# Self attention stacks as six transfers of 4 KB pieces in place of twelve of 1 KB

## What is computed

```python
def _L0_attn_ref(x, w_attn, w_proj):       # causal
    q, k, v = heads of (x @ w_attn.T)      # (8, 16, 512, 16)
    att = softmax(where(causal, q k^T / 4, -inf))
    return (att v, heads merged) @ w_proj.T

def _L1_attn_ref(x, qkv_w, proj_w, proj_b, q_norm_w, k_norm_w):
    q, k, v = heads of (x @ qkv_w.T)
    q, k = _rmsnorm(q, q_norm_w), _rmsnorm(k, k_norm_w)   # over the 16 of a head
    att = softmax(q k^T / 4)
    return (att v, heads merged) @ proj_w.T + proj_b
x = x + _L0_attn_ref(_layernorm(x), ...)
...
x = x + _L1_attn_ref(_layernorm(x), ...)
```

## Time and profile before

| | |
|---|---|
| median of 3 runs | 2481.39 us (2476.7 to 2486.93) |
| the profiled execution | 2478.18 us, its span 2476.3 us |
| granted TensorE clock, mean | 0.968 |
| TensorE busy | 2249.2 us (91%), 13992 matmuls |
| VectorE busy | 1413.6 us (57%) |
| ScalarE busy | 1188.7 us (48%) |
| GpSimd busy | 743.6 us (30%) |
| DMA | 197.00 MB in 160823 packets, 121104 of them under 2 KB |

### The profile page before, as it was taken

The page is one execution under the profiler, slowest core; times in us unless marked ns, Lnnn a source line. Parts: engine busy times, 40 slices in busy tenths (PEclk is TensorE's granted clock), DMA queues, the critical chain, the costliest instruction groups (busy, mean ns, idle before and its releaser), DMA issues. The chain is left out here.

```text
span 2476.3 us, 44303 instructions
## 1 busy us (share of the span) xinstructions
PE 2249.2 (91%) x13992; PEld 1427.4 (58%) x13993; DVE 1413.6 (57%) x3651; ACT 1188.7 (48%) x2803; POOL 743.6 (30%) x848
## 2 busy tenths in 40 slices
PE   7999999878996799899999999889985899999998
PEld 5444554344655567643333333345553799999997
DVE  4676666435874444577777777366654543434343
ACT  1666666623442463267777776533322433333332
POOL 3111111033531321233322321055430533333333
PEclk9999999989998899999999999999998999999999
DMA  6344444214221310323333333110009221222221
GB/s 162 104 131 124 130 125 125 65 39 136 83 78 43 102 53 1 90 76 103 106 94 105 99 100 99 41 33 10 10 3 375 66 38 32 38 33 37 35 36 23
DMA packets 160823, 197.00 MB, mean 80 GB/s; under 512 B 27238, under 2 KB 121104, under 8 KB 160528
## 3 DMA queue, kind: packets, MB, share of 16 engines
q1 hardware_dynamic: 145008, 175.47, 22.8%
q0 software_dynamic: 13680, 17.84, 4.5%
q10 hardware_dynamic: 1968, 1.60, 0.5%
HBM read 124.83 MB, written 70.12 MB: 79 GB/s over the span
## 5 line engine op out<-in xcount | busy, mean ns | idle before, releaser
L485 ACT ACTIVATE self_probs<-self_score_ps 128x512 f32<-128x512 f32 (+3 forms) x1024 | 479.6, 516 | 261.9 <-PE self_score_ps L856 151.9
L653 DVE TENSOR_REDUCE self_neg_max<-self_max_ps 128x1 f32<-128x512 f32 x512 | 328.6, 685 | 125.8 <-PE self_max_ps L842 122.2
L842 PE MATMUL self_max_ps<-self_k_stack,self_q_stack 96*128 96x512 bf16 (+3 forms) x1024 | 348.9, 343 | 32.9 <-DVE self_neg_max L650 21.8
L853 PE MATMUL self_score_ps<-self_q_stack,self_k_stack 99*128 99x512 bf16 (+3 forms) x1024 | 346.0, 345 | 13.4 <-ACT self_probs L485 13.2
L2758 ACT ACTIVATE x_stream<-experts_up_ps,experts_bias_now 128x128 f32<-128x128 f32 x568 | 161.9, 368 | 351.7 <-PE experts_up_ps L2970 351.7
L650 DVE CUSTOM_DVE_ANT_0 self_masked<-self_max_ps,self_later 128x128 f32<-128x128 f32 (+3 forms) x512 | 234.8, 488 | 128.0 <-PE self_max_ps L842 120.4
L2970 PEld LDWEIGHTS experts_up_ps<-experts_tileT,x_stream 128*128 128x128 f32 x2272 | 267.4, 194 | 5.2 <-issue 1.7
L2970 PE MATMUL experts_up_ps<-experts_tileT,x_stream 128*128 128x128 f32 x2272 | 267.8, 277 | 1.3 <-DVE x_stream L2880 1.3
L2980 PE MATMUL experts_down_ps<-experts_down,x_stream 128*128 x1136 | 256.8, 379 | 0.0
L853 PEld LDWEIGHTS self_score_ps<-self_q_stack,self_k_stack 99*128 99x128 bf16 x1024 | 99.3, 98 | 248.4 <-ACT self_probs L485 181.0
L867 PE MATMUL self_out_ps<-self_probs,self_values 128*32 128x512 f32 (+3 forms) x2048 | 235.1, 531 | 6.7 <-ACT self_o_raw L471 4.8
(11 more groups left out here) (339 smaller groups left out, 3783.9 us busy)
## 6 DMA issues: line engine op xcount, KB each, us to landing
self_parts_dram<-self_parts SPq DMA_DIRECT2D x64, 384.0 KB, 2.7
self_q_stack<-self_parts_dram SPq DMA_DIRECT2D x384, 64.0 KB, 2.3
self_k_stack<-self_parts_dram SPq DMA_DIRECT2D x360, 64.0 KB, 2.3
self_out_dram<-self_o_raw SPq DMA_DIRECT2D x60, 256.0 KB, 2.1
crossx_out_dram<-crossx_o_raw SPq DMA_DIRECT2D x16, 512.0 KB, 2.7
experts_up<-moe_up_dram SPq DMA_DIRECT2D x8, 1024.0 KB, 8.7
experts_down<-moe_down_dram SPq DMA_DIRECT2D x8, 1024.0 KB, 10.7
self_o_now<-self_out_dram SPq DMA_DIRECT2D x30, 256.0 KB
```

What stands on the lines that cost most here:

```text
L485: act.activation(probs[:, i % 8, 0:w], score_ps[:, (16 * n + i) % 3, 0:w], ACT.Exp).then_inc(exp_done, 1)
L653: dve.tensor_reduce(neg_max[:, n % 2, t, h:h + 1], max_ps[:, i % 2, 0:w], AX, ALU.max, negate=True).then_inc(max_read, 1)
L842: last = pe.matmul(max_ps[:, i % 2, 0:w], q_stack[0:ROWS, h, P * t:P * t + P], k_stack[0:ROWS, h, 0:w], start=True, stop=True)
L853: last = pe.matmul(score_ps[:, m % 3, 0:w], k_stack[0:KROWS, head, P * j:P * j + P], q_stack[0:KROWS, head, S - w:S], start=True, stop=not ...
```

## The change

In `lay_out` the columns of the q and k weights of both self attentions are put into the order depth, then head, within each 128 features, as the mixture of depths has them; self1's gains are repeated accordingly. The DRAM scratch is now part, feature, token. Then four heads of one depth lie together, 4 x 512 bf16 = 4 KB, and one transfer can fill three blocks of 16 rows. For q these are parts 0, 1, 2, then 0, 1, then 0; for k part 0 three times, part 1 twice, part 2 once, where the source is one part repeated along a new outermost dimension. The `stacked` semaphores count 96 an item. In self1 the sum of squares over a head can no longer use `head_ones`, whose ones are for neighbouring features; two VectorE instructions make a matrix `same_head` from the identity.

```diff
-        scratch = nc.dram_tensor(f"{name}_parts_dram", [4, P, 3, S], BF16).ap()
+        scratch = nc.dram_tensor(f"{name}_parts_dram", [4, 3, P, S], BF16).ap()
...
+        def stack_rows(half, g, which):
+
+            stk, item = (q_stack, k_stack)[which], 2 * half + which
+            heads = slice(GH * (g % 2), GH * (g % 2) + GH)
+            for r, count in ((0, 3), (3, 2), (5, 1)):
+                dst = stk[HD * r:HD * (r + count), GH * g:GH * g + GH, :].rearrange("r h t -> r (h t)")
+                if which == 0:
+                    yield dst, scratch[item, 0:count].rearrange("c (d h) t -> (c d) h t", h=8)[:, heads]
+                else:
+                    one = scratch[item, 3 - count].rearrange("(d h) t -> d h t", h=8)[:, heads].rearrange("d h t -> d (h t)")
+                    yield dst, one.unsqueeze(0).to_broadcast([count, HD, GH * S])
...
-                        wait(sp, stacked[2 * half], 192 * b)
-                        wait(sp, stacked[2 * half + 1], 192 * b)
-                        sp.dma_start(scratch[item], parts[:, item]).then_inc(parts_stored[half], 16)
+                        wait(sp, stacked[2 * half], 96 * b)
+                        wait(sp, stacked[2 * half + 1], 96 * b)
+                        sp.dma_start(scratch[item].rearrange("c p t -> p c t"), parts[:, item]).then_inc(parts_stored[half], 16)
...
-                    rows = slice((g % 2) * 64, (g % 2) * 64 + 64)
-                    for stk, item, which in ((q_stack, 2 * half, Q_PART), (k_stack, 2 * half + 1, K_PART))[0:2 if both else 1]:
-                        for r, part in enumerate(which):
-                            sp.dma_start(stk[HD * r:HD * r + HD, GH * g:GH * g + GH, :],
-                                         scratch[item, rows, part, :].rearrange("(h d) t -> d h t", d=HD)
-                                         ).then_inc(stacked[g], 16)
+                    for which in range(2 if both else 1):
+                        for dst, src in stack_rows(half, g, which):
+                            sp.dma_start(dst, src).then_inc(stacked[g], 16)
...
+                if norm:
+                    dve.tensor_reduce(one_head[:], c.ident[:].rearrange("p (d h) -> p h d", h=8), AX, ALU.max).then_inc(same_head_made, 1)
+                    dve.wait_ge(same_head_made, 1)
+                    dve.tensor_copy(same_head[:].rearrange("p (d h) -> p d h", h=8),
+                                    one_head[:].unsqueeze(1).to_broadcast([P, HD, 8])).then_inc(same_head_made, 1)
                 layer_norm(0, range(TT))
...
-                    pe.matmul(general[:, bank("s", b, i)], c.head_ones[:], squares[:, i % 2], start=True, stop=True).then_inc(ss_full, 1)
+                    pe.wait_ge(same_head_made, 2)
+                    pe.matmul(general[:, bank("s", b, i)], same_head[:], squares[:, i % 2], start=True, stop=True).then_inc(ss_full, 1)
...
-        "l0_qk": np.ascontiguousarray(qkv0[:, :2 * D]), "l0_v": np.ascontiguousarray(qkv0[:, 2 * D:]),
+        "l0_qk": np.ascontiguousarray(qkv0[:, mod_order[:2 * D]]), "l0_v": np.ascontiguousarray(qkv0[:, 2 * D:]),
...
-        "l1_qg": np.tile(a["L1_attn_q_norm_w"], P // HD).reshape(P, 1),
+        "l1_qg": np.repeat(a["L1_attn_q_norm_w"], P // HD).reshape(P, 1),
```

More of the change, by code:

```diff
@@ L149, in self_attention @@
             bias = sb("bias", [P, D])
-        scratch = nc.dram_tensor(f"{name}_parts_dram", [4, P, 3, S], BF16).ap()
+            one_head = sb("one_head", [P, 8])
+            same_head = sb("same_head", [P, P])
+        scratch = nc.dram_tensor(f"{name}_parts_dram", [4, 3, P, S], BF16).ap()
         out_scratch = nc.dram_tensor(f"{name}_out_dram", [2, 2 * GH, 2, HD, S], F32).ap()
@@ L177, in self_attention @@
         v_full, v_copied = sem("v_full"), sem("v_copied")
+        same_head_made = sem("same_head_made")
         e_full, x_biased, x_done = sem("e_full"), sem("x_biased"), sem("x_done")
@@ L543, in stack_keys @@
                     act.wait_ge(parts_stored[0], 32)
-                    for r, part in enumerate(K_PART):
-                        act.dma_start(k_stack[HD * r:HD * r + HD, GH * g:GH * g + GH, :],
-                                      scratch[1, 64 * g:64 * g + 64, part, :].rearrange("(h d) t -> d h t", d=HD)).then_inc(stacked[g], 16)
+                    for dst, src in stack_rows(0, g, 1):
+                        act.dma_start(dst, src).then_inc(stacked[g], 16)
                 transposed(0, 0)
@@ L838, in max_tile @@
                     if i == 0:
-                        pe.wait_ge(stacked[g], 192 * b + 192)
+                        pe.wait_ge(stacked[g], 96 * b + 96)
                     wait(pe, max_read, 16 * n + i - 1)
@@ L3043, in lay_out @@
         "x": a["x"],
-        "l0_qk": np.ascontiguousarray(qkv0[:, :2 * D]), "l0_v": np.ascontiguousarray(qkv0[:, 2 * D:]),
+        "l0_qk": np.ascontiguousarray(qkv0[:, mod_order[:2 * D]]), "l0_v": np.ascontiguousarray(qkv0[:, 2 * D:]),
         "l0_o": t(a["L0_attn_w_proj"]),
-        "l1_qk": np.ascontiguousarray(qkv1[:, :2 * D]), "l1_v": np.ascontiguousarray(qkv1[:, 2 * D:]),
+        "l1_qk": np.ascontiguousarray(qkv1[:, mod_order[:2 * D]]), "l1_v": np.ascontiguousarray(qkv1[:, 2 * D:]),
         "l1_o": t(a["L1_attn_proj_w"]), "l1_ob": np.tile(a["L1_attn_proj_b"], (P, 1)),
@@ L3059, in lay_out @@
         "moe_down": np.ascontiguousarray(a["L1_ffn_w_down"].transpose(0, 2, 1)), "moe_bu": np.ascontiguousarray(a["L1_ffn_b_up"].reshape(8, -1, P).transpose(2, 0, 1)), "moe_bd": np.tile(a["L1_ffn_b_down"].reshape(1, 8, D), (P, 1, 1)),
-        "l1_qg": np.tile(a["L1_attn_q_norm_w"], P // HD).reshape(P, 1),
-        "l1_kg": np.tile(a["L1_attn_k_norm_w"], P // HD).reshape(P, 1),
+        "l1_qg": np.repeat(a["L1_attn_q_norm_w"], P // HD).reshape(P, 1),
+        "l1_kg": np.repeat(a["L1_attn_k_norm_w"], P // HD).reshape(P, 1),
     }
```

## The result

The changed kernel is slower: 2516.71 us as the median of 4 runs (2501.8 to 2526.15), against 2479.91 us (2476.7 to 2486.93) for the kernel before in the same comparison. The ratio is 1.0138, with a 95% interval of 1.0096 to 1.018. The forecast was 2490 us with a range up to 2515, and 0.40 for slower by over 0.5%. So the sign of its sum (+9.0 us) was right, its size was a quarter of the measured +36.8 us, and the median lies 1.7 us above the range.

What follows compares the result with a forecast made beforehand. Compute paces both self attentions; late transfers cost 7 us (third groups), 1.6 (first opening) and 0.4 (second attention), +9.0 us on 2478.18, or 2490 us for a median. The range was 2474 to 2515 us.

Steps and rivals of the forecast that it cites:

- What bounds the kernel: Both self attentions: paced by compute, TensorE busy 94% and 98%; transfers matter only where one comes late, at three places.
- k's transfers on few engines: Stack loads: k's repeated source runs on as many engines as copies, so last data come 1.8 us later.
- The third group: First self attention, items 1 to 6: shift behind the stack 1.6 us late for TensorE, 9.6 us, taken as 7.
- From first issue to last data are 866.9 - 857.43 = 9.5 us: Time of a group's six stack transfers, read from the mixture of depths, against 7.7 us before the change.
- each piece takes a tenth more beside this stage's other traffic: Third group's upper end: k's 6.0 us become 6.6, twice in a row; 2.8 us an item, 17 us for six.
- The deduction for catching up: Third group: ScalarE and VectorE catch up during a stall, TensorE then waits less for them, so 9.6 us becomes 7.
- Openings and second attention: First opening +1.6 us, stores issued 3.7 us earlier; second attention's opening +0.4, its group 6 shift holding with 1.5 us.
- The first two engines become the bound: Rival, chance 0.16: pieces a fifth slower make each item over 4 us late; 20 to 45 us, 2512 us.
- its second sign: First-two-engines rival: the stacks of group 12 also come late for their maxima.
- the forecast's own case: First attention's third group 2 to 17 us late in all; chance 0.50, more than half of it under 12.4 us.
- Hidden anyway: Rival, chance 0.24: SP's 2.8 us and free engines offset k's delay, third group keeps its margin; -3 to +3 us, 2481.
- Fewer, larger transfers win: Rival, chance 0.10: gain at the opening's 4.86 us wait plus DMA waits and catching up; -6 us, 2475.

## Why the prediction was right and wrong

**What bounds the kernel: right.** Both attentions are paced by compute, and the loss began with transfers that were late at the places where TensorE or ScalarE has little to spare.

**k's transfers on few engines: right, and shown.** The prediction took this from the DMA share of 0.12 in the mixture of depths. In the first attention of the changed kernel, a stretch behind the issue at 186.88:

```profile
192.00:193.00 1.00, 1.00 (x12) 0.37 (x5) 0.00 (x0) 1.00 (x4) 0.00 (x0) 1.00 0.18 57
193.00:194.50 1.50, 0.90 (x9) 0.43 (x6) 1.49 (x4) 1.50 (x4) 0.14 (x1) 1.00 0.15 61
```

Shares of 0.18 and 0.15 are 2.9 and 2.4 of 16 engines at about 20 to 25 GB/s each. Two experiments show that this is the cause. With the depths outermost, the order of the stack's rows and q's source changed as well; with k six times 16 rows, both stayed as in the change. Each of the two kernels takes away all of the loss, and what they have in common is that the outermost dimension of k's source is the 16 depths and not a repetition.

The Trainium skill (DMA: Bandwidth & Descriptors, Rules for kernel authors) gives this rule, that an outermost dimension of c copies keeps a transfer to at most c engines, and its remedy, a multiple of 16 outermost. The shares agree with the rule, and the ratio of 0.9977 with the remedy. Its other rule, to coalesce transfers under 64 KB, at which bound the twelve stand, agrees in sign only once the first is kept to: 8 us by the medians between twelve and six transfers.

**The third group: mechanism, place and items right, size wrong.** The failed term is "From first issue to last data are 866.9 - 857.43 = 9.5 us", taken from the depths and left at that for this stage. In the first attention the fourth group's stack took 10.0 to 10.6 us to its landing and the first group's 10.1 to 12.3, 11.3 in the mean; the forecast gave "each piece takes a tenth more beside this stage's other traffic" only as an end of the range. The longer of the two ends, +2.8 us an item, was nearer: the items were late by 1.4 to 5.0 us, 3.7 in the mean. Item 2, the least late, fits the forecast to 0.4 us. The deduction for catching up (9.6 taken as 7) found nothing to stand on: 20.4 us of waiting made the second groups 22.1 us longer, and behind them the clock took 12.7 us more. The "20 to 25 GB/s above" in the forecast's price for the out_store has only 22 GB/s above it; the 0.7 us worked out from it held.

**The clock behind a stall: left out.** It made the 22.1 us of late shifts into 34.8 us. The stretches of the first attention in the earlier trace rows show a granted clock of 1.00. But the kernel before had one long stall, the opening's 4.86 us, and the clock fell behind it. Its stretches from 38 us on (columns as rows 2):

```profile
38.00:42.00 4.00, 1.11 (x6) 1.05 (x7) 0.34 (x3) 0.00 (x0) 0.00 (x0) 0.82 1.17 129
42.00:46.00 4.00, 4.00 (x23) 3.28 (x22) 3.23 (x13) 0.00 (x0) 0.00 (x0) 0.76 1.10 231
```

So the trace at hand showed that a stall of this length has a price behind it, and the sum put it at nothing.

**Item 0's fourth group: left out.** It cost 4.2 us in the first attention and 7.7 in the second. The forecast followed out_load at one half of an item, where TensorE waits in the end, and not the other out_load, whose sums ScalarE waits for.

**Openings and second attention: near, the latter by little.** In the first opening +1.6 us was nearly right (+2.5), though the stores came only 2.35 us earlier and not 3.7. The second attention's opening brought 0 and not +0.4. Its third groups weren't late, as forecast, but they didn't keep the 1.5 us: in items 1 to 6 the shift landed 1.1, 0.05, 0.3, 1.8, 0.5 and 0.8 us ahead of the score, where before it was 2.0 to 3.3. A little more delay would have brought the loss there too.

**Against the rivals.** "The first two engines become the bound" named 20 to 45 us and 2512 us and came nearest in size. But its mechanism was "each item is late by over 4 us", and its second sign, late stacks for the maxima, never came in the changed kernel, where half of the loss is the same late shift and the other half the clock and ScalarE's wait. It did come when the shift was issued from ScalarE's queue, in three items. So this rival's second step lies close behind the first, and the forecast's own case didn't see it. "Hidden anyway" falls by the 20.7 us row. "Fewer, larger transfers win" falls for this change; with unconfined transfers it came true at three quarters of its size (-4.4 us of -6, 2473.97 against 2478.35 us), though not in its place, since the opening gave 1.1 us of the 4.86.

**What stays open.** Why the same stack lands after 10.1 us in one item and 12.3 in another isn't known, and with it why the changed kernel's runs lie 24 us apart where those of the kernel before lie 10: many items stand near the point where a stall costs the clock as well, but no run separates that. Why TensorE still waits 3.89 us in the opening when the transfers move half as much again per microsecond wasn't tried, nor where the 8 us between twelve and six unconfined transfers lie.

## To carry to other kernels

When transfers are merged, look at the outermost dimension that the merged source has, before counting issues or bytes: a repetition there confines the transfer, and everything queued behind it on those engines, while the same repetition one level further in cost nothing here. Price a transfer that others queue behind in the stage in which it will run, and follow every wait behind it, on each engine, not only the one that was nearest to its limit. And a stall of some microseconds in a stretch that is otherwise busy costs more than its length: add what the granted clock does behind it, and look for the price in the stalls that the kernel already has.

## What the runs showed that was not expected

- The granted clock fell to 0.50 behind stalls of 2.56 to 4.60 us and stayed at 1.00 behind one of 1.25 us; six stalls of 20.4 us in all cost 12.7 us more in the groups behind them, and 12 small matmuls in each stall took these 12.7 us away.
- The out_store, itself unchanged, went from 2.1 to 6.4 us behind the confined transfers; the forecast was some 4 us.
- Two queues at once in the opening move 127 GB/s at a DMA share of 1.15 with 1 KB pieces and 188 GB/s at 1.05 with 4 KB pieces, but start the first maxima only 1.1 us earlier.
